# Two adjacency groups of rows 1 to 8 summed by TensorE instead of VectorE, in a graph and transformer layer

## The chip, the cores and the metric

The kernel runs on one core of a Trainium2 chip. The time is device microseconds of one execution of the whole program; a comparison uses the median of several runs. A profile is one further execution, recorded by the hardware profiler; it has its own time.

## The reference

`x` has 8192 rows of 128 channels, `adj` is 8192 x 8192 in fp32. A graph convolution comes first:

```python
A_hat = adj + jnp.eye(adj.shape[0], dtype=adj.dtype)
d_inv_sqrt = jnp.sum(A_hat, axis=1) ** (-0.5)
A_norm = d_inv_sqrt[:, None] * A_hat * d_inv_sqrt[None, :]
support = x @ W.T                      # x is layer-normalised before
out = jax.nn.relu(A_norm @ support)
```

The result is added to `x`. Then follows a transformer block on the layer-normalised sum: causal attention (4 heads, 2 key-value heads, 32 channels each, in rotary form) and a mixture of 8 experts with the best 2 per token. The change touches only how the row sums of `A_hat`, the degrees, are formed.

## The kernel before, in words

The adjacency is cut into 16 x 16 groups. A group (t, s) is 1 MB: 128 partitions x 4 column blocks x 512 elements, with the elements of strip t side by side in a block and the columns of strip s on the partitions and over the four blocks. `graph_stage` reads every group once in the first pass, row by row (`first_reads`), and reads those again that could be neither multiplied nor kept (`second_reads`).

A product of group (t, s) needs the scaled support of strip s (`multiply`, L566: four products of 128 x 128 weights with 512 elements, fp32, each of which the profile shows as two records). The support of strip s can be scaled only when the degree of strip s is known, that is after all 16 groups of row s have been read. So in row t the groups below the diagonal (s < t) are multiplied at once; the groups (t, t), (t, t+1), (t, t+2) are kept in six places (`keep_shared` in the profile) until their support is there; the others above the diagonal (s > t+2), called far groups here, serve only the degree in the first pass and are loaded again later. Groups that are not kept go through a ring of R = 8 places (`ring`).

The order of loads within row t is `order[t]`: the first three groups below, the far groups, the kept groups (t, t+1), (t, t+2), the other groups below, and the diagonal. SyncE issues all of them in this one order (`load_group`, L287), and a load waits until the place it goes to is free: until VectorE has added the group before (`group_summed`), and where that is multiplied in the pass, until TensorE has multiplied it too (`group_multiplied`).

VectorE adds each group into `work` (`add_group`, L367; the first one of a row is a copy, L365), so that the copy of L365 opens a row. Behind the third group of a row it scales the support of the row before (`scale_support`, L374 to L376), behind the fifth it normalises the strip of `x` (L71 to L80, L393).

TensorE follows a list written out by hand (`steps_one`). For row t: the first group below, the degree sum of row t-1 (`sum_degrees`, L593: 16 products with one column of ones, 32 records of one element; from row 8 on VectorE folds the four blocks first, and it is 4 products), the other early groups below, the three kept groups of column t-1 (`closing`), two more groups below, the transposes of the strip (`turn_norm`, L546), one more group, the support (`find_support`, L581), and the rest of the groups below. ScalarE takes the roots of the degrees (L473), copies `transposed` (L494) and the support (L496), and copies finished strips (L484).

After the first pass come the second reads, with the rest of the graph stage overlapped, and then attention and experts. In the attention stage, L1486 and L1495 are fp32 products of 128 rows into 32 columns with 256 elements, four of them into the four quarters of the partitions of one bank.

Of the kernel before, what the change touches and what calls it, by code (L numbers as in the profile page):

```python
# [25 lines left out]
P = 128  # L26
C = 128
SUB = 4
BT = SUB * P
NH, NKV, HD = 4, 2, 32  # L30
# [55 lines left out]
def graph_stage(nc, NB, dram, keep):  # L86
# [9 lines left out]
    KEPT_SPAN = 2  # L96
    NORM_AT, SCALE_AT = 4, 2
    LATE = NB // 2
    LAST = NB - 1
    stays = lambda t, s: t <= s <= t + KEPT_SPAN  # L100

    order = []
    for t in range(NB):
        below = list(range(t))
        order.append(below[:3] + [s for s in range(t + 1, NB) if not stays(t, s)]
                     + [s for s in range(t + 1, NB) if stays(t, s)] + below[3:] + [t])
    first_reads = [(t, s) for t in range(NB) for s in order[t]]
    again = {t: [s for s in range(t, NB) if not stays(t, s)] for t in range(NB)}
    resumed = [0]
    for n in range(1, NB // 2):  # L110
# [7 lines left out]
    for t in range(NB):  # L118
        early = [g for g in below_done(t)[:3] if g[1] < t - 1]
        later = below_done(t)[len(early):]  # L120
        if t:
            steps_one += early[:1] + [("degrees", t - 1)] + early[1:] + closing(t - 1)
        steps_one += later[:2] + [("turn", t)] + later[2:3] + [("support", t)] + later[3:]
    steps_two = second_reads[:1] + [("degrees", LAST)] + second_reads[1:3] + closing(LAST) + second_reads[3:]
    is_group = lambda step: not isinstance(step[0], str)
# [20 lines left out]
    with ExitStack() as ctx:  # L146
# [28 lines left out]
        root_degree = sb("root_degree", [P, SUB])  # L175
        inv_std = sb("inv_std", [P, SUB])
        ones = sb("ones", [P, 1])
        wT = sb("wT", [C, C])
        wq, wq_half = sb("wq", [C, C]), sb("wq_half", [C, C])
        wk, wk_half = sb("wk", [C, C]), sb("wk_half", [C, C])  # L180
# [11 lines left out]
        ps_degrees = ps("ps_degrees", [P, BT])  # L192
        ps_degree = ps_degrees[:, 0:SUB]
        ps_q, ps_q_half, ps_k, ps_k_half = ps_support, ps_gather[2], ps_gather[3], ps_degrees
        ps_v = ps("ps_v", [P, SUB, NKV * HD])

        ring_loaded = [sem(f"ring_loaded{s}") for s in range(R)]
        kept_loaded = [sem(f"kept_loaded{s}") for s in range(KEPT_SLOTS)]
# [18 lines left out]
        support_ready = sem("support_ready")  # L217
        support_copied = sem("support_copied")
        degree_parts = sem("degree_parts")
        degree_summed = sem("degree_summed")  # L220
        degree_root = sem("degree_root")
        support_scaled = sem("support_scaled")
# [26 lines left out]
        for g, is_again in reads:  # L249
# [11 lines left out]
            loads_of.setdefault(slot, []).append((g, is_again))  # L261
            tile_of[g, is_again] = tile
            loaded_by[g, is_again] = (semaphore, 16 * len(loads_of[slot]))
        summed = {g: n + 1 for n, g in enumerate(first_reads)}

        STACKED_BY_POOL = NB - 2

# [9 lines left out]
        @block.sync  # L277
        def _(sp):
            def load_group(g, is_again):
                earlier = replaced[g, is_again]  # L280
                if earlier is not None:
                    before, was_again = earlier
                    if not was_again:
                        sp.wait_ge(group_summed, summed[before])
                    if was_again or before[1] not in again[before[0]]:
                        sp.wait_ge(group_multiplied, produced[before])
                sp.dma_start(tile_of[g, is_again], adj[g[0], g[1]]).then_inc(loaded_by[g, is_again][0], 16)  # L287

            def load_x(t):
                if t:  # L290
                    sp.wait_ge(x_read, t)
                sp.dma_start(x_in[:], x_dram[t]).then_inc(x_loaded, 16)

            for w, d in ((wT, "wT"), (wq, "wq"), (wq_half, "wq_half"), (wk, "wk"), (wk_half, "wk_half"),
                         (wv, "wv"), (ln1, "ln1")):
                sp.dma_start(w[:], dram[d]).then_inc(weights_loaded, 16)
            load_x(0)
            for t in range(NB):
                for n, s in enumerate(order[t]):
                    load_group((t, s), False)  # L300
                    if n == NB - 4 and t < LAST:
                        load_x(t + 1)

            for n in range(2):
                sp.wait_ge(lower_stored[n], 16 * len(resumed[n::2]))
            for n, t in enumerate(resumed):
                if n >= 2:
                    sp.wait_ge(strip_gathered, n - 1)
                sp.dma_start(lower[n % 2][:], dram["lower"][t]).then_inc(lower_loaded[n % 2], 16)
                for s in again[t]:  # L310
                    load_group((t, s), True)
            for n in range(STACKED_BY_POOL, NB):
                sp.wait_ge(stack_ready, 1)
                sp.wait_ge(split_ready, 2 * n + 2)
                stack_keys(sp, n, last_stacked)
            sp.wait_ge(keys_stacked, 96 * STACKED_BY_POOL)
            sp.wait_ge(last_stacked, 96 * (NB - STACKED_BY_POOL))

        @block.gpsimd
        def _(pool):  # L320
            nc.gpsimd.memset(ones[:], 1.0).then_inc(constants_ready, 1)
            nc.gpsimd.memset(ident[:], 0.0).then_inc(constants_ready, 1)
            nc.gpsimd.memset(keep["mask_ts"][:], 0.0).then_inc(constants_ready, 1)
            nc.gpsimd.memset(keep["mask_st"][:], 0.0).then_inc(constants_ready, 1)
            nc.gpsimd.memset(keep["ones_heads"][:], 1.0).then_inc(constants_ready, 1)
            pool.wait_ge(constants_ready, 5)
            nc.gpsimd.affine_select(out=ident[:], in_=ident[:], compare_op=ALU.not_equal, fill=1.0, base=0,
                                    pattern=[[-1, P]], channel_multiplier=1).then_inc(constants_ready, 1)

            nc.gpsimd.affine_select(out=keep["mask_ts"][:], in_=keep["mask_ts"][:], compare_op=ALU.is_ge,  # L330
                                    fill=MASKED, base=0, pattern=[[-1, P]],
                                    channel_multiplier=1).then_inc(constants_ready, 1)
            nc.gpsimd.affine_select(out=keep["mask_st"][:], in_=keep["mask_st"][:], compare_op=ALU.is_ge,
                                    fill=MASKED, base=0, pattern=[[1, P]],
                                    channel_multiplier=-1).then_inc(constants_ready, 1)
            pool.wait_ge(constants_ready, 8)
            nc.gpsimd.tensor_copy(keep["ident16"][:], ident[:]).then_inc(constants_ready, 1)
            pool.wait_ge(constants_ready, 9)

            for t in range(len(resumed)):  # L340
                pool.wait_ge(strip_spilled, t + 1)
                pool.dma_start(dram["lower"][t], lower[t % 2][:]).then_inc(lower_stored[t % 2], 16)  # L342

            pool.wait_ge(group_multiplied, max(produced[g] for g in closing(LAST)))
            nc.gpsimd.memset(keep["k_stack"][SHIFT_ROW:STACK, :, :], 1.0).then_inc(stack_ready, 1)
            pool.wait_ge(stack_ready, 1)

            for n, t in enumerate(finished):
                pool.wait_ge(high_ready, n + 1)
                nc.gpsimd.tensor_tensor(q_lo[:], rotated[0][:], q_hi[:], ALU.subtract).then_inc(split_ready, 1)  # L350
                nc.gpsimd.tensor_tensor(k_lo[:], rotated[1][:], k_hi[:], ALU.subtract).then_inc(split_ready, 1)
                pool.wait_ge(split_ready, 2 * n + 2)
                if n < STACKED_BY_POOL:
                    stack_keys(pool, n, keys_stacked)

        @block.vector
        def _(dve):
# [21 lines left out]

            for t in range(NB):  # L380
                for n in range(NB):
                    add_group(t, n)
                    if t and n == SCALE_AT:
                        scale_support(t - 1)
                    if n == NORM_AT:
# [80 lines left out]
        def _(act):  # L466
# [19 lines left out]
            for t in range(NB):  # L486
                if t:
                    root_degrees(t - 1)
                if t > KEPT_SPAN:
# [5 lines left out]
                act.wait_ge(support_ready, t + 1)  # L495
                nc.scalar.copy(support[:, t * SUB:(t + 1) * SUB, :],  # L496
                               ps_support[:].rearrange("p (s c) -> p s c", s=SUB)).then_inc(support_copied, 1)
            root_degrees(LAST)

            def load_strip(n):  # L500
# [13 lines left out]
            for n, t in enumerate(finished):  # L514
# [11 lines left out]
                act.wait_ge(h_turned, n + 1)  # L526
                nc.scalar.mul(hT, ps_turn[:], ln1[:, 0:1]).then_inc(h_copied, 1)
                act.wait_ge(v_ready, n + 1)
                nc.scalar.copy(keep["v"][:, t * SUB:(t + 1) * SUB, :], ps_v[:]).then_inc(v_copied, 1)
                act.wait_ge(high_ready, n + 1)  # L530
                if n + 1 < NB:
                    load_tables(n + 1)
# [9 lines left out]
        def _(pe):  # L542
# [4 lines left out]
                last.then_inc(signal, 1)  # L547

            pe.wait_ge(weights_loaded, 16 * 7)
            pe.wait_ge(constants_ready, 9)  # L550

            def multiply(g, is_again):
                t, s = g
# [31 lines left out]
            def sum_degrees(t):  # L585
                pe.wait_ge(degree_parts, t + 1)
                if t:
                    pe.wait_ge(degree_root, t)
                parts = 1 if t >= LATE else SUB
                total = reduced[t % 2] if t >= LATE else partial_degree[t % 2]  # L590
                for s in range(SUB):
                    for c in range(parts):
                        last = nc.tensor.matmul(ps_degree[:, s:s + 1], total[:, c * BT + s * P:c * BT + (s + 1) * P],  # L593
                                                ones[:], start=(c == 0), stop=(c == parts - 1))
                last.then_inc(degree_summed, 1)

            def turn_strip(n):
                t = finished[n]
# [27 lines left out]
                    last = nc.tensor.matmul(ps_v[:, s, :], hT[:, s * P:(s + 1) * P], wv[:], start=True, stop=True)  # L626
                last.then_inc(v_ready, 1)

            pieces = {"degrees": sum_degrees, "turn": turn_norm, "support": find_support}
            for step in steps_one:  # L630
                if is_group(step):
                    multiply(step, False)
# [1410 lines left out]
```

## Time and profile before

| | |
|---|---|
| median of 3 runs | 3518.84 us (3518.19 to 3521.54) |
| profiled execution | 3524.27 us, its span 3522.5 us |
| TensorE busy | 3085.2 us (88%) |
| VectorE busy | 2554.2 us (73%) |
| ScalarE busy | 1423.8 us (40%) |
| GpSimd busy | 1728.2 us (49%) |
| first pass over the adjacency | from 4.6 us (first load) to about 867 us (last degree) |

The span is cut into times from its first instruction. PE is TensorE, PEld its weight loads, DVE VectorE, ACT ScalarE, POOL GpSimd; SPq is the queue from which SyncE issues transfers. A line such as `3.60 PE L566 MATMUL ... x8` merges neighbouring instructions of one kind: its length and their number. The bracket behind it is the idle time of the engine before it and what ended that. PEclk is the mean clock that TensorE was granted, 1.00 being 2.4 GHz and 0.50 being 1.2 GHz.

### The profile page before, as it was taken

How to read it: one execution, taken by the hardware profiler on the slowest of the kernel's cores; microseconds unless marked ns; L12 is line 12 of the kernel's file. 1: busy time of each engine (PE TensorE's matmuls, PEld its weight loads, DVE VectorE, ACT ScalarE, POOL GpSimd, SP SyncE). 2: the span in 40 equal slices, each digit the busy share in tenths (PEclk: the TensorE clock that was granted, in tenths of full speed). 3: DMA queues.
4: the chain of work that ended last, by engine and by line, in shares of the span. 5: the costliest groups of instructions: out<-in, count | busy, mean ns of one | idle time of the engine just before them, and what ended most of it. 6: DMA issues, size and time to landing. Idle time of an engine off the chain costs nothing. (4 is left out here: it accounts for less than half of the span.)

```text
span 3522.5 us, 56503 instructions
## 1 busy us (share of the span) xinstructions
PE 3085.2 (88%) x22241; PEld 1353.5 (38%) x22241; DVE 2554.2 (73%) x2736; ACT 1423.8 (40%) x2843; POOL 1728.2 (49%) x1113
## 2 busy tenths in 40 slices
PE   2678889899989987998999999999999999957992
PEld 1334434344434432433433333333333333324661
DVE  8888887675554455779878977877987898616773
ACT  0000000000000003666666666666666666745661
POOL 0000000000321113776888699877699869763665
PEclk9778999999999997999999999999999999988996
DMA  9898876678667944440000000000000000002224
GB/s 376 349 391 366 349 308 267 282 296 302 254 261 292 359 155 167 160 164 13 29 18 18 7 24 17 11 8 7 7 17 18 11 2 17 9 26 93 74 74 154
DMA packets 157501, 506.75 MB, mean 144 GB/s; under 512 B 20081, under 2 KB 66298, under 8 KB 112326
## 3 DMA queue, kind: packets, MB, share of 16 engines
q1 hardware_dynamic: 111400, 448.58, 32.9%
q10 hardware_dynamic: 33024, 31.47, 2.7%
q0 software_dynamic: 12816, 23.11, 2.0%
q8 instruction: 179, 2.93, 0.3%
q14 instruction: 82, 0.67, 0.1%
HBM read 426.31 MB, written 75.37 MB: 142 GB/s over the span
## 5 line engine op out<-in xcount | busy, mean ns | idle before, releaser
L1223 DVE TENSOR_REDUCE unit_max<-ps_max 128x2 f32<-128x1024 f32 (+2 forms) x1088 | 1225.9, 1171 | 297.4 <-PE ps_max L1452 254.1
L998 POOL TENSOR_TENSOR chunk_sum<-chunk_sum,probs 128x1024 f32<-128x1024 f32 x480 | 1132.3, 2359 | 287.8 <-ACT probs L1093 277.1
L1093 ACT ACTIVATE probs<-ps_ring 128x512 f32<-128x512 f32 x2112 | 1089.8, 596 | 440.2 <-PE ps_ring L1471 408.1
L566 PE MATMUL ps_gather<-ring,keep_attended 128*128 128x512 f32 x1688 | 789.8, 625 | 140.1 <-DMA ring<-in_adj 121.4
L1471 PE MATMUL ps_ring<-q_stack,keep_shared 97*128 97x512 f16 x2112 | 673.9, 385 | 27.7 <-ACT probs L1093 22.2
L1486 PE MATMUL ps_acc<-probs,keep_shared 128*32 128x256 f32 (+1 forms) x8448 | 566.8, 386 | 0.0
L566 PEld LDWEIGHTS ps_gather<-ring,keep_attended 128*128 128x128 f32 x1688 | 332.6, 202 | 541.7 <-issue 541.7
L367 DVE TENSOR_TENSOR work<-work,ring 128x2048 f32<-128x2048 f32 x195 | 446.6, 2290 | 34.5 <-DMA ring<-in_adj 30.7
L342 POOL DMA_DIRECT2D scratch_lower<-lower x13 | 7.3, 560 | 805.0 <-ACT lower L484 805.0
L1452 PE MATMUL ps_max<-k_heads,q_heads 32*128 32x512 f16 (+3 forms) x2176 | 276.0, 378 | 69.9 <-DVE unit_max L1223 48.5
L1495 PE MATMUL ps_acc<-probs,keep_ones_heads 128*32 128x256 f32 (+1 forms) x4224 | 327.9, 380 | 0.0
L1471 PEld LDWEIGHTS ps_ring<-q_stack,keep_shared 97*128 97x128 f16 x2112 | 163.5, 98 | 407.7 <-ACT probs L1093 252.0
L1486 PEld LDWEIGHTS ps_acc<-probs,keep_shared 128*32 128x32 f32 x8448 | 222.2, 110 | 244.4 <-issue 121.8
L1744 POOL DMA_INDIRECT scratch_parts<-moe_y_rows,moe_y_index x156 | 168.5, 1080 | 126.5 <-DVE moe_y_rows L1862 87.9
L1452 PEld LDWEIGHTS ps_max<-k_heads,q_heads 32*128 32x128 f16 x2176 | 73.4, 91 | 339.0 <-DVE unit_max L1223 195.5
L350 POOL TENSOR_TENSOR q_lo<-rotated,q_hi 128x512 f16<-128x512 f32 x16 | 18.4, 1151 | 337.0 <-DVEq L460 337.0
L1495 PEld LDWEIGHTS ps_acc<-probs,keep_ones_heads 128*32 128x32 f32 x4224 | 138.0, 111 | 87.7 <-issue 4.1
L566 PE MATMUL ps_gather<-keep_shared,keep_attended 128*128 128x512 f32 x360 | 160.9, 603 | 2.5 <-DVE keep_attended L376 2.5
L367 DVE TENSOR_TENSOR work<-work,keep_shared 128x2048 f32<-128x2048 f32 x45 | 103.1, 2292 | 79.4 <-DMA keep_shared<-in_adj 78.8
L1038 POOL DMA_INDIRECT scratch_slots<-batch_rows,keep_slot_index x120 | 118.8, 990 | 38.1 <-POOL chunk_sum L998 26.0
L473 ACT ACTIVATE root_degree<-ps_degrees 128x4 f32<-128x4 f32 x16 | 2.8, 173 | 324.3 <-PE ps_degrees L593 324.3
L1878 DVE SCALAR_TENSOR_TENSOR moe_hidden<-moe_ps_up,moe_gate 114x512 f32<-114x512 f32 (+1 forms) x117 | 80.9, 691 | 64.0 <-ACT moe_gate L1786 62.8
(243 smaller groups left out, 2667.5 us busy)
## 6 DMA issues: line engine op xcount, KB each, us to landing
ring<-in_adj SPq DMA_DIRECT2D x302, 1024.0 KB, 13.9
keep_shared<-in_adj SPq DMA_DIRECT2D x45, 1024.0 KB, 10.8
scratch_slots<-empty_rows SPq DMA_DIRECT2D x16, 2080.0 KB, 14.3
moe_x_rows<-scratch_slots SPq DMA_DIRECT2D x39, 260.0 KB, 2.7
moe_parts<-scratch_parts SPq DMA_DIRECT2D x32, 256.0 KB, 4.2
x_in<-in_x SPq DMA_DIRECT2D x16, 256.0 KB, 13.3
x_in<-in_x ACTq DMA_DIRECT2D x16, 256.0 KB, 7.5
work<-in_cos ACTq DMA_DIRECT2D x16, 256.0 KB, 4.1
```

The lines of the kernel that those rows point to most:

```text
L367: add = nc.vector.tensor_tensor(total, total, tile_of[g, False], ALU.add)
L566: last = nc.tensor.matmul(bank[:], support[:, s * SUB + c, :], tile_of[g, is_again][:, c * BT:(c + 1) * BT], start=(first and c == 0), sto ...
L998: steps.then(nc.gpsimd.tensor_tensor(totals, totals, weights, ALU.add))
L1038: pool.indirect_dma_start(dram["slots"], bass.IndirectOffsetOnAxis(slot_index[:, at, k:k + 1], 0), rows_of(b)[:, at // SUB, at % SUB, k, : ...
L1093: nc.scalar.activation(probs[:, q % SLOTS, i, kv, :, lo:], halves(bank)[:, :, lo:], ACT.Exp, scale=SCALE).then_inc(ring_read, 1)
L1223: nc.vector.tensor_reduce(unit_max[:, half % 2, heads, s % 2, unit], ps_max[:, base:base + HEADS, at:at + width], AX_X, ALU.max).then_inc( ...
L1452: last = nc.tensor.matmul(ps_max[:, base + n, at:at + width], q_heads[rows, T % 2, s * P:(s + 1) * P], k_heads[rows, G * BT:G * BT + width ...
L1471: last = nc.tensor.matmul(out[:, :, lo:], k_stack[0:STACK, kv, G * BT + j * P:G * BT + (j + 1) * P], q_stack[:, T % QBUF, H, kv * NREP:(kv ...
L1486: nc.tensor.matmul(ps_acc[h * HD:(h + 1) * HD, lo:HALF], values[:, G * SUB + j, kv * HD:(kv + 1) * HD], probs[:, q % SLOTS, i, kv, h % NRE ...
L1495: last = nc.tensor.matmul(ps_acc[at * HD:(at + 1) * HD, HALF + lo:], keep["ones_heads"][:], probs[:, q % SLOTS, i, 1, r, lo:], start=False ...
L1744: pool.indirect_dma_start(dram["parts"], bass.IndirectOffsetOnAxis(y_index[:, g % BUFFERS, s:s + 1], 0), y_rows[:, g % BUFFERS, s, :], Non ...
L1878: nc.vector.scalar_tensor_tensor(out=hidden[0:width, k % HB], in0=ps_up[k % 2][0:width, :], scalar=HIDDEN_SCALE / (TOKEN_SCALE * WEIGHT_SC ...
```

## The change

In rows 1 to 8 the first two far groups, `by_rows[t]`, are no longer added by VectorE. TensorE sums them over the partitions with weights `first_ones` (128 x 32, ones in the first column, zeros elsewhere): per group four products, one per column block, each into its own quarter of 32 partitions of a bank `ps_rows`. All four use the same weights. ScalarE copies the bank to `row_sums` behind the support copy of the row, and `sum_degrees` takes it in with four more products with the column of ones. In TensorE's list the new step `("rows", t)` stands right behind the degree sum of row t-1. The place of such a group is free for the next load when TensorE has summed both (`rows_summed`), and `ps_v` now shares the bank of `ps_rows`. Two more constants are set by GpSimd at the start.

```diff
+    ROWS_TO, TAKEN = 9, 2
+    by_rows = {t: [s for s in order[t] if s > t and not stays(t, s)][:TAKEN] for t in range(1, ROWS_TO)}
...
-            steps_one += early[:1] + [("degrees", t - 1)] + early[1:] + closing(t - 1)
+            steps_one += early[:1] + [("degrees", t - 1)] + [("rows", t)] * (t in by_rows) + early[1:] + closing(t - 1)
...
-                    if not was_again:
+                    if not was_again and by_products(*before):
+                        sp.wait_ge(rows_summed, rows_taken[before[0]])
+                    elif not was_again:
                         sp.wait_ge(group_summed, summed[before])
...
-                    add_group(t, n)
+                    if not by_products(t, order[t][n]):
+                        add_group(t, n)
...
+                if t in by_rows:
+                    act.wait_ge(rows_summed, rows_taken[t])
+                    nc.scalar.copy(row_sums[:], ps_rows[:]).then_inc(rows_copied, 1)
...
+                if t in by_rows:
+                    pe.wait_ge(rows_copied, rows_taken[t])
                 for s in range(SUB):
                     for c in range(parts):
                         last = nc.tensor.matmul(ps_degree[:, s:s + 1], total[:, c * BT + s * P:c * BT + (s + 1) * P],
-                                                ones[:], start=(c == 0), stop=(c == parts - 1))
+                                                ones[:], start=(c == 0), stop=(c == parts - 1 and t not in by_rows))
+                    if t in by_rows:
+                        last = nc.tensor.matmul(ps_degree[:, s:s + 1], row_sums[:, s * P:(s + 1) * P], ones[:],
+                                                start=False, stop=True)
...
+            def sum_rows(t):
+                if rows_taken[t] > 1:
+                    pe.wait_ge(rows_copied, rows_taken[t] - 1)
+                for n, s in enumerate(by_rows[t]):
+                    pe.wait_ge(*loaded_by[(t, s), False])
+                    for c in range(SUB):
+                        last = nc.tensor.matmul(ps_rows[c * HD:(c + 1) * HD, :], first_ones[:],
+                                                tile_of[(t, s), False][:, c * BT:(c + 1) * BT],
+                                                start=(n == 0), stop=True, skip_group_check=True)
+                last.then_inc(rows_summed, 1)
```

## Rows read from the trace of the kernel before

**Rows 1.** Windows, rows 3 to 8, then 2 and 1; columns as the header.
```profile
core 0: us, PE busy (x) PEld busy (x) DVE busy (x) ACT busy (x) POOL busy (x), PEclk, DMA share, GB/s
140.78:192.18 51.40, 31.98 (x92) 16.83 (x92) 40.16 (x27) 2.03 (x5) 0.77 (x1) 0.73 0.83 338
192.18:240.69 48.51, 39.26 (x105) 20.09 (x106) 40.16 (x26) 2.03 (x5) 0.56 (x1) 0.77 1.00 403
240.69:284.62 43.93, 35.91 (x96) 17.53 (x94) 40.16 (x26) 1.25 (x4) 0.54 (x1) 0.81 0.93 373
284.62:330.06 45.44, 38.55 (x112) 19.33 (x113) 40.17 (x27) 2.24 (x6) 0.54 (x1) 0.89 0.88 359
330.06:378.71 48.65, 42.04 (x120) 20.70 (x119) 40.15 (x26) 2.04 (x5) 0.54 (x1) 0.86 0.86 349
378.71:434.24 55.53, 48.47 (x147) 24.32 (x146) 43.78 (x28) 2.62 (x6) 0.54 (x1) 0.94 0.84 341
95.28:140.78 45.50, 22.43 (x76) 12.41 (x76) 40.17 (x26) 1.55 (x4) 0.00 (x0) 0.73 0.92 374
52.17:95.28 43.11, 17.80 (x60) 11.99 (x60) 40.16 (x26) 1.55 (x4) 0.00 (x0) 0.80 0.93 381
```
**Rows 2.** Waits of SyncE's queue, 0 to 720 us: total, times, longest.
```profile
SPq L286 <- PE ps_gather L566: 477.1, 63, 34.8
SPq L287 <- DVE work L367: 70.3, 49, 5.3
```
**Rows 3.** Order of time of SyncE's queue: start, length, what.
```profile
69.52 2.46 SPq L287 DMA_DIRECT2D ring<-in_adj  x5
...
312.36 24.43 SPq L287 DMA_DIRECT2D ring<-in_adj  x9
355.47 0.80 SPq L287 DMA_DIRECT2D keep_shared<-in_adj  x2
```
**Rows 4.** Windows of 4 us in rows 1, 3 and 7; columns as in rows 1.
```profile
68.00:72.00 4.00, 1.96 (x8) 0.78 (x6) 3.90 (x6) 0.21 (x1) 0.00 (x0) 1.00 0.33 92
...
168.00:172.00 4.00, 3.71 (x12) 1.64 (x10) 3.93 (x3) 0.26 (x1) 0.00 (x0) 1.00 0.00 0
...
350.00:354.00 4.00, 4.00 (x11) 1.77 (x10) 2.38 (x4) 0.69 (x2) 0.54 (x1) 1.00 0.02 6
```
**Rows 5.** Order of time of TensorE in rows 1 and 2.
```profile
60.40 5.59 PE L566 MATMUL ps_gather<-keep_shared,keep_attended 128*128 128x512 f32 x8 [1.27 <-DVE keep_attended L376]
65.83 3.60 PE L566 MATMUL ps_gather<-ring,keep_attended 128*128 128x512 f32 x8
...
105.28 8.78 PE L566 MATMUL ps_gather<-keep_shared,keep_attended 128*128 128x512 f32 x16 [1.27 <-DVE keep_attended L376]
```
**Rows 6.** Order of time of TensorE in row 7, last line row 8.
```profile
336.22 3.63 PE L593 MATMUL ps_degrees<-ones,work 128*128 128x1 f32 x32
339.71 8.81 PE L566 MATMUL ps_gather<-ring,keep_attended 128*128 128x512 f32 x16
348.36 10.46 PE L566 MATMUL ps_gather<-keep_shared,keep_attended 128*128 128x512 f32 x24
365.44 10.09 PE L566 MATMUL ps_gather<-ring,keep_attended 128*128 128x512 f32 x16 [6.61 <-DMA ring<-in_adj]
...
390.48 7.11 PE L566 MATMUL ps_gather<-ring,keep_attended 128*128 128x512 f32 x16
```
**Rows 7.** Order of time of VectorE at the turn from row 6 to 7.
```profile
327.62 2.29 DVE L367 TENSOR_TENSOR work<-work,keep_shared 128x2048 f32<-128x2048 f32 x1
...
340.99 4.61 DVE L367 TENSOR_TENSOR work<-work,ring 128x2048 f32<-128x2048 f32 x2
```
**Rows 8.** The page's costliest groups: VectorE's adds from the ring.
```profile
L367 DVE TENSOR_TENSOR work<-work,ring 128x2048 f32<-128x2048 f32 x195 | 446.6, 2290 | 34.5 <-DMA ring<-in_adj 30.7
```
**Rows 9.** Order of time of TensorE in the attention stage.
```profile
2007.09 1.07 PE L1486 MATMUL ps_acc<-probs,keep_shared 128*32 128x256 f32 x16
2007.98 0.61 PE L1495 MATMUL ps_acc<-probs,keep_ones_heads 128*32 128x256 f32 x8
2008.52 0.61 PE L1471 MATMUL ps_ring<-q_stack,keep_shared 97*128 97x512 f16 x2
```

More of the change, by code:

```diff
@@ L177, in graph_stage @@
         ones = sb("ones", [P, 1])
+        first_ones = sb("first_ones", [P, HD])
+        row_sums = rotated[0]
         wT = sb("wT", [C, C])
@@ L194, in graph_stage @@
         ps_q, ps_q_half, ps_k, ps_k_half = ps_support, ps_gather[2], ps_gather[3], ps_degrees
-        ps_v = ps("ps_v", [P, SUB, NKV * HD])
+        ps_rows = ps("ps_rows", [P, BT])
+        ps_v = ps_rows[:, 0:SUB * NKV * HD].rearrange("p (s c) -> p s c", s=SUB)
         ring_loaded = [sem(f"ring_loaded{s}") for s in range(R)]
@@ L219, in graph_stage @@
         degree_parts = sem("degree_parts")
+        rows_summed = sem("rows_summed")
+        rows_copied = sem("rows_copied")
         degree_summed = sem("degree_summed")
@@ L263, in graph_stage @@
             loaded_by[g, is_again] = (semaphore, 16 * len(loads_of[slot]))
-        summed = {g: n + 1 for n, g in enumerate(first_reads)}
+        by_products = lambda t, s: t in by_rows and s in by_rows[t]
+        summed = {g: n + 1 for n, g in enumerate(g for g in first_reads if not by_products(*g))}
+        rows_taken = {t: n + 1 for n, t in enumerate(sorted(by_rows))}
         STACKED_BY_POOL = NB - 2
@@ L321, in _ @@
             nc.gpsimd.memset(ones[:], 1.0).then_inc(constants_ready, 1)
+            nc.gpsimd.memset(first_ones[:, 0:1], 1.0).then_inc(constants_ready, 1)
+            nc.gpsimd.memset(first_ones[:, 1:HD], 0.0).then_inc(constants_ready, 1)
             nc.gpsimd.memset(ident[:], 0.0).then_inc(constants_ready, 1)
@@ L325, in _ @@
             nc.gpsimd.memset(keep["ones_heads"][:], 1.0).then_inc(constants_ready, 1)
-            pool.wait_ge(constants_ready, 5)
+            pool.wait_ge(constants_ready, 7)
             nc.gpsimd.affine_select(out=ident[:], in_=ident[:], compare_op=ALU.not_equal, fill=1.0, base=0,
@@ L335, in _ @@
                                     channel_multiplier=-1).then_inc(constants_ready, 1)
-            pool.wait_ge(constants_ready, 8)
+            pool.wait_ge(constants_ready, 10)
             nc.gpsimd.tensor_copy(keep["ident16"][:], ident[:]).then_inc(constants_ready, 1)
-            pool.wait_ge(constants_ready, 9)
+            pool.wait_ge(constants_ready, 11)
             for t in range(len(resumed)):
@@ L528, in _ @@
                 act.wait_ge(v_ready, n + 1)
-                nc.scalar.copy(keep["v"][:, t * SUB:(t + 1) * SUB, :], ps_v[:]).then_inc(v_copied, 1)
+                nc.scalar.copy(keep["v"][:, t * SUB:(t + 1) * SUB, :], ps_v).then_inc(v_copied, 1)
                 act.wait_ge(high_ready, n + 1)
@@ L549, in _ @@
             pe.wait_ge(weights_loaded, 16 * 7)
-            pe.wait_ge(constants_ready, 9)
+            pe.wait_ge(constants_ready, 11)
             def multiply(g, is_again):
@@ L627, in project @@
                 last.then_inc(v_ready, 1)
-            pieces = {"degrees": sum_degrees, "turn": turn_norm, "support": find_support}
+            pieces = {"degrees": sum_degrees, "turn": turn_norm, "support": find_support, "rows": sum_rows}
             for step in steps_one:
```

## The prediction

> **What bounds the kernel now.** I read the page first, then the busy time of each engine in the stretches between two copies of VectorE (one copy opens each row of groups), then who the SyncE queue waited for, then the order of time of SyncE, TensorE and VectorE inside single rows. The change touches only the first pass over the adjacency, rows 1 to 9 of 16, that is 52 to 440 us of the span.
>
> The stretches of rows 1 to 8 last 43.1 to 55.5 us each [rows 1]. In each VectorE is busy some 40 us and the DMA engines 83 to 100% of the time. VectorE looks like the bound in rows 1 and 2 (40.2 of 43.1 us), so taking adds from it looks like a gain. It is not, and the reader has to see why in the queue of loads. SyncE issues all adjacency loads in one order, and stands still until the place a load goes to is free. It waited 477.1 us for TensorE's products and 70.3 us for VectorE's adds [rows 2]. What counts is which of these waits leaves the DMA engines empty.
>
> - Row 1: SyncE goes on at 69.52 us [rows 3], 0.1 us after TensorE is through with the ring group of row 1, which runs from 65.83 us for 3.60 us [rows 5]. In 68 to 72 us the DMA engines are busy 33% [rows 4].
> - Row 3: in 168 to 172 us they are idle altogether, VectorE is busy 3.93 of 4 us with what had already landed, and TensorE is busy 3.71 us with the group whose place the next load needs [rows 4].
> - Row 7: SyncE issues nine ring loads from 312.36 us and then nothing until 355.47 us [rows 3]. TensorE began the 24 records of the kept products (three groups of eight) at 348.36 us, 0.43 us each [rows 6], so 355.47 us is just after the second group, and that product frees the place. The DMA engines move almost nothing in 350 to 354 us [rows 4]. TensorE gets its next group at 365.44 us after 6.61 us of idle time [rows 6], 10.0 us after SyncE went on.
>
> So one ring of causes sets each row: a group lands, TensorE goes through its list to the kept products (or to the next ring group), that frees a place, SyncE issues, the DMA engines, now empty, need some 10 us in rows 4 and later, or the rest of the row in rows 1 to 3, until TensorE's next group is there. VectorE stands beside this ring: its last add for row 6 ends at 329.91 us, and TensorE asks for that row's degree at 336.22 us [rows 6, 7]. It is ahead in the other rows from 2 to 9 too. Behind row 9 nothing makes it up: TensorE's list in the second reads and all later stages wait for this pass, so a shift here is a shift of the end.
>
> **The change part by part.**
>
> *Taken from VectorE.* Two adds in each of rows 1 to 8, 16 of 2.29 us [rows 8], 36.6 us of work. I value this at nothing, as VectorE ends ahead of its reader everywhere but at the degree of row 0, which is not changed. Its end would count only if VectorE were the one to free the place that SyncE is stuck on. It also frees the two places no later: they now wait for TensorE's sum, but the loads that need them stand in the queue behind a load that waits for a later product. The scaling of the support and the normalisation move forward in VectorE's list; TensorE waits for the scaling 1.27 us in rows 1 and 2 [rows 5] and not at all in rows 3 to 9.
>
> *New sums of groups on TensorE.* Per row 2 groups x 4 products of 128 rows into 32 columns, 512 elements, in fp32, which shows as 2 records each: 16 records. The four products of a group write different quarters of the partitions. The nearest rows are those of the attention stage, the same form with 256 elements: 16 records take 0.89 us (2007.09 to 2007.98 us), against 16 x 0.21 = 3.4 us had they run one by one at half of the 0.43 us of a full 512-element record [rows 6, 9]. So four run at once. With twice the elements 16 records take 1.78 us. The next 8 records in that stage take 0.54 us until the following form starts, where 0.445 us would be in line [rows 9]: 0.1 us for leaving the form, and I take as much for entering it. That gives 2.0 us a row. The bounds: 0.9 us, if the elements were hidden by something that paces the 256-element records, and 6.9 us, if the four ran one after the other (16 x 0.43 us). I take 2.0 us, from the same form. On this the Trainium skill speaks against the change: "TensorE: Matmul & The Clock Gate", section Measured speedup vs the span model, gives three column tiles only 2.38 times the speed of one, so a fifth is lost. By that, estimated, the 6.9 us would shrink to 2.2 us instead of 1.78, and the sum below would be some 3 us larger. The trace has 3.8 times for four tiles, and I follow it. "TensorEngine Tiling", section Key Properties, adds that a change of the tiling mode drains the engine; the 0.1 us above is what this trace shows of that.
>
> *Degree sums.* Four products more, 8 records, in the degrees of rows 1 to 8 (done in rows 2 to 9). 32 such records take 336.22 to 339.71 us, 3.49 us, 0.109 us each [rows 6], so 0.87 us. They wait for ScalarE's copy of the sums, which stands behind the support copy of the same row; ScalarE is busy 1.3 to 2.6 us in a row of 43 to 56 us [rows 1], so this wait is over 10 us and more before. Bounds 0 and 1.7 us (low clock).
>
> *The wait for the loads.* The new step stands in TensorE's list ahead of the row's second and third ring group and the kept products, and with it SyncE. In row 7 VectorE adds the first two of these groups from 340.99 us without waiting for a load [rows 7], and TensorE would ask at 339.71 + 0.87 = 340.6 us; the loads come 2.5 us apart there. I take no wait; up to 1 us a row is possible.
>
> *What lies on the path.* In rows 1 and 2 the new step covers the 1.27 us wait for the scaling. Row 1: 2.0 us, up to 4.0 at the low clock, less 1.27: 1.4. Row 2: 0.87 + 2.0 - 1.27 = 1.6. Rows 3 to 8: 2.87 each, 17.2. Row 9: 0.9. Together 21.1 us.
>
> *The clock.* Of TensorE's two levels (1.2 and 2.4 GHz) rows 1 to 7 show the lower one right after the degree sums, whose records of one element keep the engine little occupied: the 16 records after them take 8.65 us in row 7 (339.71 to 348.36 us) and 7.1 us in row 8, where it stayed high [rows 6]. The difference, 1.6 us, is the price of one such drop. With 40 records instead of 32 a drop is likelier in row 8 and may be longer elsewhere: between -3 us (the new products keep the engine busy and spare some drops) and +13 us (one more in each of eight rows). I take +4.
>
> Sum: +25 us. The profiled execution took 3524.3 us (span 3522.5 and 1.8 around it), which gives 3549; the median of the runs is 5.4 us lower, and against that the forecast is 3518.8 + 25 = 3544 us, 0.7% slower.
>
> **The rivals.**
>
> *Beside the path.* TensorE idles 6.6 us in each of rows 5 to 9 [rows 6], and the new work might come out of that idle time. That holds where the loads after the gap are limited by the stream of earlier loads. For it: the DMA engines are busy 100% in row 4 [rows 1], so that there the empty stretch is under 1 us. Against it: the engines are empty before each of the other restarts [rows 4]. If it held everywhere, only a few us remain: 3520 (3515 to 3526).
>
> *VectorE is the bound.* If its adds were what lets the loads go on, each of rows 1 to 8 would be shorter by its two adds, 4.6 us, but no more than the DMA engines are idle in the row (the time of the row times one less the share, rows 1): 3.0, 3.6, 4.6, 0, 3.1, 4.6, 4.6 and 4.6 us for rows 1 to 8, 28 us. 3491 us, or some 3500 with the degree sums taken off. For it: VectorE's 40 of 43 us in row 1, and SyncE's 70 us behind it. Against it: in each empty stretch read above VectorE had its adds behind it or was working on landed groups, and SyncE went on with a product of TensorE. It decides for the faster side if more than half of the 25 us of added path are outweighed by rows whose restart hangs on an add.
>
> *The four products don't run together.* Then 6.9 instead of 1.8 us, 5.1 us more in eight rows: +41, 3585 us. For it only that all four write the same bank, but so do those of the attention stage, which do run together.
>
> *The clock falls in every row.* +9 on the forecast: 3553 us. It lies within the forecast's own range.
>
> **How the numbers follow.** About 0.2% (7 us) is what a measurement tells from no change. The forecast with the clock case holds 71%: 3544 us, own range 3532 to 3558. Beside the path 12%, VectorE the bound 10%, the serial products 7%. Of the first, some 2% fall within 7 us of before. Faster 0.12, same 0.13, slower 0.75. The range from 3518 to 3562 leaves out the serial case, the VectorE case and the edges.
>
> **What would show it.** Right: the new records take 1.8 to 2.1 us a row at the high clock; degree sums of 40 records at 4.4 us; VectorE's idle time in rows 1 to 8 up by about the 36.6 us taken plus the delay; the gap before TensorE's first ring group after the kept products still 6.6 us; the copy that opens row 9 some 19 to 23 us later than at 434.24, and the later stages moved as a block. Wrong: that copy at or before 434 us, or the empty stretches of the DMA engines shorter than before, or the new records at 0.43 us each.

## The result, and the profile after

The changed kernel is slower: 3537.06 us (median of 5 runs) against 3521.54 us of before, ratio 1.0054, 95% interval 1.0041 to 1.0067. On 3521.5 us that is +19 us (+14 to +24); the two medians themselves lie 15.5 us apart, inside that interval. The forecast was +25 us, with a range from -1 to +43.

The page of the changed kernel, its engines and VectorE's adds from the ring (before: 195 of them, 446.6 us, [rows 8]):

```profile
span 3535.3 us, 56872 instructions
PE 3103.2 (88%) x22433; PEld 1361.5 (39%) x22433; DVE 2514.9 (71%) x2720; ACT 1428.5 (40%) x2851; POOL 1728.6 (49%) x1115
L380 DVE TENSOR_TENSOR work<-work,ring 128x2048 f32<-128x2048 f32 x179 | 410.0, 2290 | 42.0 <-DMA ring<-in_adj 38.7
```

VectorE lost the 36.6 us of work that the change takes from it. Between the copies that open rows 1 and 9 it idles 113.4 us instead of 57.2, that is 56.2 us more: the 36.6 us, and the 19.5 us by which these rows together grew. Who SyncE's queue waited for, 0 to 740 us (total, times, longest); for the kernel before, the totals of [rows 2] are the same up to 740 us. TensorE is still the one:

```profile
SPq L297 <- PE ps_gather L583: 494.5, 63, 34.8
SPq L298 <- DVE work L380: 67.9, 46, 5.5
```

The order of time of TensorE in row 7, from the start of the degree sum of row 6 (its other parts are left out) to the first group after the kept products, with the queue of SyncE (start, length, what), as in [rows 3, 6]:

```profile
345.15 0.95 PE L612 MATMUL ps_degrees<-ones,work 128*128 128x1 f32 x8
...
350.42 3.64 PE L625 MATMUL ps_rows<-ring,first_ones 128*32 128x512 f32 x16
353.99 7.85 PE L583 MATMUL ps_gather<-ring,keep_attended 128*128 128x512 f32 x16
361.68 10.46 PE L583 MATMUL ps_gather<-keep_shared,keep_attended 128*128 128x512 f32 x24
378.75 9.10 PE L583 MATMUL ps_gather<-ring,keep_attended 128*128 128x512 f32 x16 [6.61 <-DMA ring<-in_adj]
```
```profile
322.19 23.53 SPq L298 DMA_DIRECT2D ring<-in_adj  x9
368.78 0.80 SPq L298 DMA_DIRECT2D keep_shared<-in_adj  x2
```

The degree sum takes 5.27 us (345.15 to 350.42) where it took 3.49. The new records take 3.57 us. The two groups behind them take 7.69 us where they took 8.65. The kept products last as long as before, SyncE goes on just after the second of them, and the wait of TensorE is 6.61 us as in [rows 6]. The windows of the changed kernel around these steps (columns as in [rows 1]) show the new step at 1.2 GHz, and the DMA engines empty while TensorE works towards the kept products:

```profile
349.00:355.00 6.00, 6.00 (x24) 2.50 (x25) 3.88 (x9) 0.17 (x1) 0.00 (x0) 0.50 1.01 421
359.00:363.00 4.00, 4.00 (x11) 1.74 (x10) 0.00 (x0) 0.00 (x0) 0.00 (x0) 1.00 0.01 6
```

In the second window VectorE does nothing: in row 7 it waits 8.9 us for a root from ScalarE. Row 5 shows the same; VectorE in its order of time:

```profile
255.56 2.28 DVE L380 TENSOR_TENSOR work<-work,ring 128x2048 f32<-128x2048 f32 x1
266.94 0.18 DVE L406 RECIPROCAL inv_std<-std 128x4 f32<-128x4 f32 x1 [9.10 <-ACT std L506]
```

It gets to the normalisation 9.1 us before ScalarE has the root (2.77 us in the same row of the kernel before), which stands in ScalarE's list behind the copy of a strip that TensorE finishes with a kept product. Over rows 1 to 8 VectorE's waits for the two roots of ScalarE grow from 28.5 to 81.2 us. The relief turns into idle time.

The last degree of the first pass (ScalarE's root), in the kernel before and the changed one:

```profile
867.26 0.17 ACT L473 ACTIVATE root_degree<-ps_degrees 128x4 f32<-128x4 f32 x1 [34.54 <-PE ps_degrees L593]
```
```profile
887.34 0.17 ACT L487 ACTIVATE root_degree<-ps_degrees 128x4 f32<-128x4 f32 x1 [34.53 <-PE ps_degrees L612]
```

The pass ends 20.1 us later. The spans of these two executions differ by 12.8 us only; what is missing lies mainly in the attention stage, 1772.4 instead of 1781.3 us from its first to its last product with `probs`. No run edits that stage. Among the traces of all 13 kernels it takes 1771.6 to 1781.3 us, and the 23 runs of the kernel before in the comparison of `relief_only` lie 14.6 us apart, so that this may be scatter. But the three kernels without the new step have the longest attention stages (1781.0 to 1781.3 us), and a small gain there from the change is not excluded. So below the end of the first pass and the ratio are read together.

### The profile page after: what moved, and what is told of

The parts are those of the page before. It is cut to its first block and busy times, and to the rows that moved or that the text cites. A ratio compares the mean times of both kernels' runs of the same rounds, so it can differ in the third digit from the quotient of the medians.

```text
span 3535.3 us, 56872 instructions
## 1 busy us (share of the span) xinstructions
PE 3103.2 (88%) x22433; PEld 1361.5 (39%) x22433; DVE 2514.9 (71%) x2720; ACT 1428.5 (40%) x2851; POOL 1728.6 (49%) x1115
## 5 line engine op out<-in xcount | busy, mean ns | idle before, releaser
L1504 PE MATMUL ps_ring<-q_stack,keep_shared 97*128 97x512 f16 x2112 | 672.1, 384 | 26.8 <-ACT probs L1126 21.6
L380 DVE TENSOR_TENSOR work<-work,ring 128x2048 f32<-128x2048 f32 x179 | 410.0, 2290 | 42.0 <-DMA ring<-in_adj 38.7
```

The costliest lines, as they stand in the source:

```text
L380: add = nc.vector.tensor_tensor(total, total, tile_of[g, False], ALU.add)
L1504: last = nc.tensor.matmul(out[:, :, lo:], k_stack[0:STACK, kv, G * BT + j * P:G * BT + (j + 1) * P], q_stack[:, T % QBUF, H, kv * NREP:(kv ...
```

## The experiments

Theory P: TensorE's own list, with the loads released by its kept products, sets the length of each row, and VectorE stands beside it. Rival V: VectorE's adds hold the loads back, so that its relief gives time back. All ratios are to the kernel before, with runs on the same chip. A distance to the changed kernel, where it is read from ratios, is the difference of two such ratios and uncertain by some 6 us. Rows 9 to 15, in which the kernels differ in nothing but the degree sum of row 8, take 432.9 to 436.6 us in the traces, so that ends of the first pass are uncertain by some 4 us. In all diffs `-` is the changed kernel, where no other is named.

**Only the relief of VectorE** (`relief_only`), on the kernel before:

```diff
+    ROWS_TO, TAKEN = 9, 2
...
+    left_out = {(t, s) for t in range(1, ROWS_TO) for s in [s for s in order[t] if s > t and not stays(t, s)][:TAKEN]}
...
-                    if not was_again:
+                    if not was_again and before in left_out:
+                        sp.wait_ge(*loaded_by[before, False])
+                    elif not was_again:
                         sp.wait_ge(group_summed, summed[before])
...
-                    add_group(t, n)
+                    if (t, order[t][n]) not in left_out:
+                        add_group(t, n)
```


> The kernel before, with the 16 far groups loaded but neither added by VectorE nor summed by TensorE (the degrees of rows 1 to 8 lack them). Theory P (TensorE's list sets the rows, VectorE stands beside it): no change, within 2 us of before, ratio 0.9995 to 1.0005, and the products of row 9 at the same time as before within 2 us. Rival V (VectorE's adds let the loads go on): faster by up to 28 us, ratio 0.992 to 0.997.

Measured 3524.81 against 3523.42 us, ratio 1.0005 (0.9995 to 1.0015). 36.6 us of VectorE's work gone, the places of these groups free as soon as they have been loaded, and no gain: rival V falls. In its trace VectorE waits 36.8 us longer for ScalarE's two roots in rows 1 to 8, which is just the work that it was spared, and the two waits of 1.27 us of TensorE for the scaling stay. The first pass ends at 871.45 us, 4.2 us later than before, and TensorE's first group behind the kept products of row 9 stands 3.5 us later, more than the 2 us expected; that is in the size of the scatter between executions.

**Only the work of TensorE** (`products_only`):

```diff
-        summed = {g: n + 1 for n, g in enumerate(g for g in first_reads if not by_products(*g))}
+        summed = {g: n + 1 for n, g in enumerate(first_reads)}
...
-                    elif not was_again:
+                    if not was_again:
                         sp.wait_ge(group_summed, summed[before])
...
-            nc.gpsimd.memset(first_ones[:, 0:1], 1.0).then_inc(constants_ready, 1)
+            nc.gpsimd.memset(first_ones[:, 0:1], 0.0).then_inc(constants_ready, 1)
...
-                    if not by_products(t, order[t][n]):
-                        add_group(t, n)
+                    add_group(t, n)
```


> The changed kernel, but VectorE adds all groups as before and TensorE does all the new work too, on weights that are all zero, so that the new sums add nothing. Theory P: as slow as the changed kernel, 16 to 22 us over before, ratio 1.0045 to 1.0065. Rival V (VectorE's relief gave back part of the price): slower than the changed kernel by the part given back, up to 28 us, ratio up to 1.013.

Ratio 1.0064 (1.0045 to 1.0083); first pass until 887.17 us, as in the changed kernel (887.34). The whole price is TensorE's. The two first passes agree to 0.2 us, the ratios only within some 8 us: that far the relief gives nothing back.

**The new step without its part in the degree** (`no_degree`):

```diff
-                    if t in by_rows:
-                        last = nc.tensor.matmul(ps_degree[:, s:s + 1], row_sums[:, s * P:(s + 1) * P], ones[:],
-                                                start=False, stop=True)
```


> The changed kernel without the four products that take the sums of the far groups into the degree (the degrees of rows 1 to 8 lack them); the new step itself stays. Theory P: 0.9 us less in rows 2 to 9, 7 us, and up to 3 us more if low clock stretches get shorter: 7 to 10 us under the changed kernel, ratio 1.0025 to 1.0035. A rival (the new step at its place costs all, the longer degree sum nothing): equal to the changed kernel, 1.005.

Ratio 1.0027 (1.0016 to 1.0037), 9.5 us less than the changed kernel, the first pass 10.8 us shorter (until 876.53 us). Half of the loss goes with the 64 records of one element.

**Four groups instead of two** (`taken4`):

```diff
-    ROWS_TO, TAKEN = 9, 2
+    ROWS_TO, TAKEN = 9, 4
```


> The changed kernel with four far groups a row instead of two. Theory P: two more groups are 16 records more in each of rows 1 to 8 on TensorE's list, 1.8 us at the high clock and 3.6 at the low one, nothing back from VectorE, plus waits for the later of the four groups' loads (2.5 us apart): 14 to 35 us over the changed kernel, ratio 1.009 to 1.015. Rival V: VectorE's relief doubles too, and the time stays within 5 us of the changed kernel.

Ratio 1.0105 (1.0091 to 1.012), +18 us on the changed kernel, the first pass until 909.40 us, +22.1. It grows with TensorE's records, as theory P has it.

**The step behind the kept products** (`rows_later`):

```diff
-            steps_one += early[:1] + [("degrees", t - 1)] + [("rows", t)] * (t in by_rows) + early[1:] + closing(t - 1)
+            steps_one += early[:1] + [("degrees", t - 1)] + early[1:] + closing(t - 1) + [("rows", t)] * (t in by_rows)
```


> The changed kernel with the new step behind the kept products instead of ahead of them: there the engine runs at its high clock and then idles 6.6 us a row for a load. Theory P: the 16 records take 1.8 us instead of 3.6 and lie in the idle time of rows 3 to 8; what stays on the path is the longer degree sum, 0.9 us in eight rows, and its effect on the clock: 7 to 10 us over before, ratio 1.002 to 1.003. A rival (any work on TensorE in these rows costs its length, wherever it stands): 16 us or more over before, ratio 1.0045 and up.

Ratio 1.0052 (1.0037 to 1.0068): no gain, and my expectation missed. (The profiled execution was the slowest of the six runs, 3551.62 us; its first pass lasts until 894.98 us, 7.6 us longer than in the changed kernel.) The trace of this kernel in row 7 (TensorE) shows the part that held, 1.9 us for the records and 4.8 us of idle time left instead of 6.6:

```profile
371.50 10.46 PE L583 MATMUL ps_gather<-keep_shared,keep_attended 128*128 128x512 f32 x24
381.89 1.92 PE L625 MATMUL ps_rows<-ring,first_ones 128*32 128x512 f32 x16
388.64 9.82 PE L583 MATMUL ps_gather<-ring,keep_attended 128*128 128x512 f32 x16 [4.83 <-DMA ring<-in_adj]
```

SyncE's queue in row 4, first the kernel before, then this one, shows the part that I had left out:

```profile
208.88 4.24 SPq L287 DMA_DIRECT2D ring<-in_adj  x3
219.19 0.33 SPq L287 DMA_DIRECT2D keep_shared<-in_adj  x1
```
```profile
208.46 25.50 SPq L298 DMA_DIRECT2D ring<-in_adj  x4
234.04 0.39 SPq L298 DMA_DIRECT2D keep_shared<-in_adj  x1
```

In row 4 the load of the last far group takes the place of the first summed one. It now waits for the step behind the kept products (over at 233.5 us), and the kept loads wait behind it. TensorE gets its next group later for it, first the kernel before, then this one:

```profile
231.07 5.58 PE L566 MATMUL ps_gather<-ring,keep_attended 128*128 128x512 f32 x8 [8.53 <-DMA ring<-in_adj]
```
```profile
248.52 6.47 PE L583 MATMUL ps_gather<-ring,keep_attended 128*128 128x512 f32 x8 [14.96 <-DMA ring<-in_adj]
```

So the step has two costs: its time in TensorE's list and the moment at which it lets go of two places. The first is paid in rows 1 to 3 all the same, since there a ring group follows the kept products without a gap; my expectation counted row 3 among the rows with one. From copy to copy, rows 1, 2 and 5 are 3.2, 4.6 and 3.3 us longer than in the changed kernel, rows 6, 7 and 8 are 0.8, 2.1 and 3.8 us shorter.

**Split by rows** (`rows_split`): the step at its place in rows 1 to 4, behind the kept products in rows 5 to 8.

```diff
-            steps_one += early[:1] + [("degrees", t - 1)] + [("rows", t)] * (t in by_rows) + early[1:] + closing(t - 1)
+            steps_one += early[:1] + [("degrees", t - 1)] + [("rows", t)] * (t in by_rows and t < 5) + early[1:] + closing(t - 1) + [("rows", t)] * (t in by_rows and t >= 5)
```


> The changed kernel with the new step at its place in rows 1 to 4 and behind the kept products in rows 5 to 8. Theory S (the step moved back cost in rows 1 to 4, where the loads that reuse the places of the far groups were next in SyncE's queue, and was hidden in rows 5 to 8): row 4's kept loads issued near 222 us as in the changed kernel and not at 234, and rows 5 to 8 each 2 to 3.5 us shorter than in it; 7 to 11 us under the changed kernel, ratio 1.002 to 1.0035. Rival (the work costs its length wherever it stands): as the changed kernel, 1.0045 to 1.006.

Ratio 1.0021 (1.001 to 1.0031), 12 us under the changed kernel, just past the 7 to 11 us expected; the first pass, until 881.27 us, is 6.1 us shorter. The first kept load of row 4 goes out at 223.73 us and not at 234: that part of theory S holds. Rows 5 to 8 are 2.0, 0.9, 1.5 and 4.0 us shorter than in the changed kernel, less evenly than the 2 to 3.5 us each that it had, though inside its range in sum. The rival, the ratio of the changed kernel, falls.

**Ahead of the degree sum** (`rows_first`):

```diff
-            steps_one += early[:1] + [("degrees", t - 1)] + [("rows", t)] * (t in by_rows) + early[1:] + closing(t - 1)
+            steps_one += early[:1] + [("rows", t)] * (t in by_rows) + [("degrees", t - 1)] + early[1:] + closing(t - 1)
```


> The changed kernel with the new step ahead of the degree sum of the row before instead of behind it. Theory C (a low stretch of the clock follows the degree sum and has its own length, whatever work falls into it): the new records take 1.9 us at the high clock where they took 3.6, but the groups behind the degree sum now run low, and the row is as long as in the changed kernel, within 1 us a row; ratio 1.004 to 1.0065. Rival (the new records cost 3.6 us only because they stand behind the degree sum): 1.7 us less in each of rows 5 to 8 and 1 us in rows 2 to 4, 8 to 10 us under the changed kernel, ratio 1.002 to 1.003. In both the step may wait up to 3 us for its loads in rows 2 to 4.

Ratio 1.0131 (1.0117 to 1.0146): both theories missed. (The profiled execution, 3585.74 us, was the slowest of four runs; the others took 3571 to 3574 us.) The new records among the groups of instructions of this kernel, 0 to 500 us (busy, mean ns, then idle before and what ended it), and row 8 of TensorE:

```profile
L625 PE MATMUL ps_rows<-ring,first_ones 128*32 128x512 f32 x128 | 19.7, 689 | 36.7 <-DMA ring<-in_adj 36.7
```
```profile
439.42 1.06 PE L625 MATMUL ps_rows<-ring,first_ones 128*32 128x512 f32 x8 [0.29 <-DMA ring<-in_adj]
441.81 1.06 PE L625 MATMUL ps_rows<-ring,first_ones 128*32 128x512 f32 x8 [1.33 <-DMA ring<-in_adj]
442.81 1.20 PE L612 MATMUL ps_degrees<-ones,work 128*128 128x1 f32 x8
...
450.70 8.65 PE L583 MATMUL ps_gather<-ring,keep_attended 128*128 128x512 f32 x16
```

The step asks for its groups before they have landed. Of its 36.7 us of waiting, 20.5 us stand in row 1, where TensorE idled 19.3 us before its degree sum anyway; the other 16.2 us, up to 4.3 us a row, are new. In row 8 the records run at the high clock, but the degree sum takes 7.9 us and the two groups after it 8.5, where they took 4.9 and 8.1 in the changed kernel. That the low stretch has a length of its own is not shown; it became longer, in rows where short idle times stand ahead of it. The copy that opens row 9 comes 43.4 us later than in the changed kernel, so that the new waits are less than half of the loss, and what the clock by itself costs stays open.

**Fewer records in the degree.** The `no_degree` run points at the records of one element. In the kernel before VectorE folds the four blocks from row 8 on; here it does so in all rows (`LATE = 0` in place of `NB // 2`), in the kernel before (`fold_before`), in the changed one (`fold_after`), in the changed one with the step behind the kept products (`fold_later`), and in the changed one with `ROWS_TO, TAKEN = 3, 2`, so that TensorE sums far groups in rows 1 and 2 alone (`fold_two_rows`). The edits of the last one:

```diff
-    LATE = NB // 2
-    ROWS_TO, TAKEN = 9, 2
+    LATE = 0
+    ROWS_TO, TAKEN = 3, 2
```

> The kernel before with VectorE folding the four blocks in all rows (LATE = 0), so that every degree sum on TensorE has 8 records instead of 32. Theory P: 24 records of 0.109 us less, 2.6 us, and one drop of the clock less, up to 1.6 us, in rows 1 to 8: 15 to 30 us faster. VectorE gets 3.7 us more in rows 0 to 7, which shows as a wait of TensorE for the degree in the first rows. Ratio 0.991 to 0.996. Rival (VectorE becomes the bound): no gain or slower.

> The changed kernel with VectorE folding in all rows (LATE = 0): 16 records in the degree sums of rows 1 to 8 instead of 40. Theory P: the new sums are back on the path at 1.8 us a row (high clock) and 0.9 for the degree, so 10 to 20 us over the folded kernel before, but under the kernel before: ratio 0.994 to 0.999. VectorE's relief has a value here only as far as the folded kernel before shows TensorE waiting for the degree.

> As fold_after, with the new step behind the kept products. Theory P: the new sums lie in the idle time; only the longer degree sum, 0.9 us a row, stands against VectorE's relief. 5 to 10 us under fold_after, ratio 0.991 to 0.997; whether it beats fold_before says whether the relief is worth more than 7 us once VectorE folds.

> VectorE folds in all rows (LATE = 0), and TensorE sums far groups in rows 1 and 2 alone. In the folded kernel before, TensorE waits 4.85 and 4.22 us there for VectorE's scaling, in no later row. Theory P: these are the only rows in which the relief is worth anything; the waits go, and rows 3 to 8 are as in the folded kernel before: 4 to 6 us under it, ratio 0.991 to 0.994. Rival: the new sums cost as much as the waits did, ratio 0.994 to 0.9955.

| | ratio | 95% interval | first pass ends at |
|---|---|---|---|
| `fold_before` | 0.9941 | 0.9928 to 0.9954 | 850.40 us |
| `fold_after` | 0.9987 | 0.9976 to 0.9997 | 862.67 us |
| `fold_later` | 0.9962 | 0.9947 to 0.9977 | 858.52 us |
| `fold_two_rows` | 0.9922 | 0.991 to 0.9934 | 846.60 us |

All four ratios came as theory P had them, `fold_later` within its band but above `fold_before`. In `fold_after`, whose degree sums are shorter, TensorE asks earlier for the groups of the new step and waits for their loads in three rows (0.72, 1.34 and 2.35 us), so that its 16 us over `fold_before` are not the price of the records alone. In the folded kernels VectorE is late. TensorE in rows 1 and 2, first of `fold_before`, then of `fold_two_rows`:

```profile
62.20 5.65 PE L566 MATMUL ps_gather<-keep_shared,keep_attended 128*128 128x512 f32 x8 [4.85 <-DVE keep_attended L376]
...
107.40 8.68 PE L566 MATMUL ps_gather<-keep_shared,keep_attended 128*128 128x512 f32 x16 [4.22 <-DVE keep_attended L376]
...
142.89 6.25 PE L566 MATMUL ps_gather<-ring,keep_attended 128*128 128x512 f32 x8 [21.11 <-DMA ring<-in_adj]
```
```profile
57.62 3.64 PE L625 MATMUL ps_rows<-ring,first_ones 128*32 128x512 f32 x16
61.19 4.28 PE L583 MATMUL ps_gather<-keep_shared,keep_attended 128*128 128x512 f32 x8
...
102.60 1.92 PE L625 MATMUL ps_rows<-ring,first_ones 128*32 128x512 f32 x16
104.45 7.13 PE L583 MATMUL ps_gather<-keep_shared,keep_attended 128*128 128x512 f32 x16
...
138.46 6.57 PE L583 MATMUL ps_gather<-ring,keep_attended 128*128 128x512 f32 x8 [21.13 <-DMA ring<-in_adj]
```

The waits for the scaling are gone, and row 3 begins 4.4 us earlier. VectorE in row 1, again first of `fold_before`, shows that it is the relief and not only the cover by the new step:

```profile
61.24 0.18 DVE L374 RECIPROCAL inv_sqrt_degree<-root_degree 128x4 f32<-128x4 f32 x1
```
```profile
58.00 0.18 DVE L387 RECIPROCAL inv_sqrt_degree<-root_degree 128x4 f32<-128x4 f32 x1 [1.10 <-ACT root_degree L487]
```

In `fold_before` the scaling stands behind two adds that `fold_two_rows` does not have, and begins 3.2 us later. `fold_two_rows` is the fastest kernel of the study, 27 us under the one before. Its interval touches that of `fold_before` (0.991 to 0.9934 against 0.9928 to 0.9954), so that its lead of 4 to 7 us over it rests on the trace as well (first pass 3.8 us shorter).

Rows 1 and 2 are not the only ones in which VectorE is near its limit once it folds: in `fold_before` rows 4 to 7 last 44.6 to 44.7 us each with VectorE busy 43.7 to 43.8 us, and TensorE waits 0.21 and 1.34 us for the folded sum in two of them. What the relief alone would be worth there no run shows.

## Why the prediction was right

- *What bounds the rows.* Right: the waits of SyncE, TensorE's idle times behind the kept products and the empty DMA stretches are where they were, and the experiments that take the relief and the work apart give 1.0005 and 1.0064. (These idle times are 6.5 to 7.6 us in rows 5 to 9 of the kernel before, and not 6.6 us in each.) From row 9 on the copies stay 19.3 to 21.8 us late: nothing makes the shift up within the pass.
- *Taken from VectorE: nothing.* Right, by `relief_only`. What I had not named is where it goes: into waits for ScalarE's roots.
- *The new records, 2.0 us a row.* Right at the high clock (1.9 us in `rows_later`), so four run at once. In the changed kernel they took 26.8 us over the eight rows, with one wait of 0.25 us, and 3.57 us in each of rows 5 to 8, as they fall into the low stretch behind the degree sum. That is 11 us more than the 16 us I had. But the groups behind them, which had run low before, gained: over rows 1 to 8 they took 10.0 us less (in row 7, 7.69 instead of 8.65 us). So the net 16.8 us meet the term, but two shifts of the clock had to cancel for that. The sum allowed for spared drops with 3 us at most; that they would make up for the slow records was luck.
- *The degree sums, 0.87 us.* 8.8 us over rows 2 to 9 instead of 7, and unevenly: they grew by some 0.1 us or less in rows 3 and 4, where they had run partly low before (4.34 and 4.41 us), and by up to 2.5 us in rows 5 to 8, where they now do (6.0 us in row 6). The sign of 4.4 us for 40 records shows in rows 2 to 4 (4.45 us) and in none of rows 5 to 8 (4.9 to 6.0).
- *The loads.* Right: one wait of 0.25 us, in row 4.
- *The cover in rows 1 and 2.* Right: both waits of 1.27 us are gone.
- *The clock, +4.* The term that was off. The sum of the steps is 26.8 + 8.8 - 10.0 - 2.5 = 23.1 us, against 21.1 us without the clock: it cost about 2 us. The drop that I had called likelier in row 8 came: the two groups there took 8.10 instead of 6.95 us. The groups behind the long idle times of rows 2 to 9 differ by up to 1.1 us a row either way and are 1.9 us shorter in sum; with that the 20.1 us are met but for about 1 us.
- *The copy that opens row 9*, forecast 19 to 23 us later than 434.24, stands at 453.52 us, +19.3. "The later stages moved as a block" did not hold in this pair of executions, for the attention stage above all.
- *The rivals.* "VectorE is the bound" falls with `relief_only`. "Beside the path" falls with the ratio of the change, and `rows_later` shows what it would take: the step has to stand in the gap itself, not merely in a row that has one. The serial products fall with the 1.9 us. "The clock falls in every row" came half true: the new records or the groups behind them ran low in every one of rows 1 to 8, but the price was 2 us and not 13, since low stretches had been there in seven of these rows before.

## What to carry to other kernels

An engine that is busy 93% of a row can still be beside the path; what tells is who releases the load that the empty DMA engines wait for. Work moved from it to the engine that does the releasing cost about its full length here, unless it stood in that engine's own gap, and there it must not hold places that the next loads need. Look first at what the releasing engine does inefficiently (here records of one element): moving that work the other way gave 0.6%, and then the relief of VectorE had a value as well, in the two rows where TensorE waited for its scaling.

## What the runs showed of the hardware

- 16 fp32 records of 128 rows into 32 columns with 512 elements, in four quarters of one bank, take 1.9 us at the high clock and 3.57 us at the low one: at the high clock that is 3.6 times as fast as 16 such records one after the other would be, by the 0.43 us of a full record (6.9 us).
- Behind the 32 or 40 one-element records of a degree sum TensorE mostly ran at the low clock for a while, and the work that stood there first took it: the new records in the changed kernel (3.57 us in rows 5 to 8), the ring groups in the kernel before (8.65 us in row 7). It is no rule without exception: in row 8 of the kernel before the two groups behind 32 such records took 6.95 us, at the high clock. With 8 records instead of 32 (`fold_before`) the two groups behind them took 6.95 us in each of rows 4 to 8, where the kernel before has 9.39 us in row 4. Low stretches also stood behind short waits: in row 7 of `fold_after` TensorE waited 2.35 us for a load, and the 16 records of the next two groups took 8.66 us.
